# A row of reciprocals by TensorE, q scaled in PSUM, and five banks for the first words of the MLP

## The reference

```python
x   = x.reshape(4096, 512)                       # 2 batches of 2048 tokens
xn  = (x - mean(x)) / sqrt(var(x) + 1e-5)
q   = xn @ Wq.T + bq;  k = ctx @ Wk.T + bk;  v = ctx @ Wv.T + bv   # ctx: 2 x 77 x 512
a   = softmax(q k.T / sqrt(32)) v                # 16 heads of 32
x1  = x + tanh(g_xattn) * (a @ Wo.T + bo)
x1n = layernorm(x1)
sx  = max|x1n| / 127;  s1 = max|W1| / 127        # one scale per tensor
h   = gelu((round(x1n/sx) @ round(W1/s1).T + b1) * s1*sx)          # 2048 wide
sh  = max|h| / 127;   s2 = max|W2| / 127
out = x1 + tanh(g_ffn) * ((round(h/sh) @ round(W2/s2).T + b2) * s2*sh)
```

## Time and profile before

| | us |
|---|---|
| median of 3 runs | 666.09 |
| lowest and highest | 665.76 and 668.17 |
| the profiled execution | 664.78 |
| its span, first to last instruction | 662.6 |

### The profile page before, as it was taken

One profiled execution on the slowest core, in us unless ns is written; L12 is line 12 of the kernel. 1 busy time (PEld: TensorE's weight loads), 2 busy tenths in 40 slices (PEclk: granted clock), 3 DMA queues, 4 the chain that ended last, 5 costly groups with the idle time before them and its releaser, 6 DMA issues. The chain is left out here.

```text
span 662.6 us, 9249 instructions
## 1 busy us (share of the span) xinstructions
PE 593.2 (90%) x3289; PEld 336.4 (51%) x3311; DVE 452.0 (68%) x634; ACT 334.9 (51%) x400; POOL 288.6 (44%) x240
## 2 busy tenths in 40 slices
PE   6977869595998999969799997899999999999997
PEld 6832534452654746536457566544444454444443
DVE  5934861592784887827738688498999869893271
ACT  2445244463346364452462723577777669665440
POOL 3349366098076481872842522000000535843272
PEclk8997959796998999979989998999999999999999
DMA  8457020215321221121200103887777779797764
GB/s 316 155 194 236 1 80 1 47 64 175 125 97 35 47 97 35 32 80 47 96 1 0 66 0 137 302 307 279 285 267 276 321 317 320 282 403 307 240 232 181
DMA packets 45926, 107.42 MB, mean 162 GB/s; under 512 B 6976, under 2 KB 7744, under 8 KB 41280
## 3 DMA queue, kind: packets, MB, share of 16 engines
q1 hardware_dynamic: 44544, 105.55, 44.3%
q10 hardware_dynamic: 1344, 1.37, 0.6%
HBM read 64.95 MB, written 41.96 MB: 161 GB/s over the span
## 5 line engine op out<-in xcount | busy, mean ns | idle before, releaser
L1384 PE MATMUL ps<-h_sb,w_q 128*128 (+1 forms) x476 | 108.7, 379 | 2.4 <-ACT xo L1447 1.8
L1650 PE MATMUL ps<-w_q,h_q 128*128 128x512 bf16 x441 | 96.5, 379 | 0.4
L1108 POOL TENSOR_TENSOR xr<-xr,row 128x512 f32<-128x512 f32 x28 | 37.3, 1344 | 108.9 <-DMA xr<-in_x_t 89.2
L1732 POOL TENSOR_TENSOR xo<-xo,b2s 128x512 f32<-128x512 f32 x32 | 57.3, 1821 | 61.3 <-DMA xo<-x_dram 42.8
L1384 PEld LDWEIGHTS ps<-h_sb,w_q 128*128 128x128 bf16 x488 | 46.7, 98 | 53.9 <-ACT xo L1447 2.4
L684 ACT ACTIVATE prob<-ps 77x1024 f32<-77x1024 f32 x64 | 61.7, 1014 | 23.4 <-PE ps L466 18.9
L1650 PEld LDWEIGHTS ps<-w_q,h_q 128*128 128x128 bf16 x448 | 43.8, 98 | 52.9
L1447 ACT ACTIVATE xo<-ps,b1s,sc 128x1024 f32<-128x1024 f32 x48 | 57.6, 1204 | 20.0 <-PE ps L1384 19.0
L505 PE MATMUL ps<-wo_hi,c_lo 128*128 128x512 f32 x112 | 46.1, 412 | 23.6 <-POOL c_lo L1142 23.6
L1518 DVE TENSOR_REDUCE hmax<-xo 128x1024 f32 (+1 forms) x48 | 57.0, 1212 | 9.6 <-ACT xo L1447 9.4
L424 PE MATMUL ps<-xt_hi,wq_hi 128*128 128x512 f32 x128 | 53.2, 415 | 8.4 <-DVE x L913 7.7
(11 more groups left out here) (163 smaller groups left out, 1158.2 us busy)
## 6 DMA issues: line engine op xcount, KB each, us to landing
h_dram<-xo SPq DMA_DIRECT2D x48, 512.0 KB, 2.8
h_sb<-h_dram SPq DMA_DIRECT2D x16, 1024.0 KB, 11.1
x_dram<-x SPq DMA_DIRECT2D x8, 1024.0 KB, 4.1
xo<-x_dram SPq DMA_DIRECT2D x8, 1024.0 KB, 5.1
x<-h_dram SPq DMA_DIRECT2D x8, 1024.0 KB, 8.0
x<-in_x SPq DMA_DIRECT2D x7, 1024.0 KB, 5.6
xr<-in_x_t SPq DMA_DIRECT2D x28, 256.0 KB, 4.0
out<-xo SPq DMA_DIRECT2D x7, 1024.0 KB, 5.9
```

Source lines behind the costliest of these rows:

```text
L1108: nc.gpsimd.tensor_tensor(xa, xa, row[:], ALU.mult).then_inc(xr_mul, 1)
L1384: mm = nc.tensor.matmul(ps[:, 2 * (m % 2) + s, :], w1_q[:, k, m * P:(m + 1) * P], xq_t[:, one(2 * j + s), k, :], start=(k == 0), stop=(k = ...
L1650: mm = nc.tensor.matmul(ps[:, 4 * s + t, :], h_q[s][:, m, t * P:(t + 1) * P], w2_q[:, m, :], start=(m == 0), stop=(m == MF - 1))
L1732: nc.gpsimd.tensor_tensor(xo[:, s, t, :], xo[:, s, t, :], b2s[:], ALU.add).then_inc(xb_on, 1)
```

## The change

In attention:

- `pass_rstd`, the DRAM buffer and `scale_xt` are gone. TensorE's `row_turn(n)` turns the four columns of `rstd1`, broadcast, into a bank (`BC`, for n = 1 `BS`), in step n-1 behind the third `scores_by_token`. ScalarE's `row_copy(n)` copies the bank to `row`. `transpose_max` and, in step 0, the second half of v wait for that copy.
- x is split unscaled (`xt_high` waits for the DMA alone). VectorE's `q_scale(c, m)` multiplies the q in its PSUM bank by `row`, in place, before `q_high` and `q_low` read it. `divide(i-1, 0)` moves behind the last `token_max`.
- The maximum of w1 is turned by TensorE and reduced by VectorE, which does `w1_scale` before the residuals.
- In step 0 `weight_means` moves one place forward and ScalarE's copy of it from m = 1 to m = 0.
- A Gelu of one column stands in ScalarE's `last_steps`.

In hidden, the first eight tiles go through five banks, three are copied by VectorE; the last product of the last step, its Gelu and its maximum are done by halves. In output a factor that rounding doesn't need is computed after the first rounding.

```diff
-                def pass_rstd(c):
-                    sp.wait_ge(ln1_rstd, rstd_value(c))
-                    sp.dma_start(sh.rstd_dram[c].rearrange("(t p) -> p t", p=P), rstd1[:],
-                                 allow_slow_non_contiguous=True).then_inc(row_out, 16)
-                    sp.wait_ge(row_out, 16 * c)
-                    if c >= 2:
-                        sp.wait_ge(xr_mul, KD * (c - 1))
-                    sp.dma_start(row[:], as_row(sh.rstd_dram[c]).to_broadcast([P, CH])).then_inc(row_in, 16)
...
+                def row_turn(n):
+
+                    pe.wait_ge(ln1_rstd, rstd_value(n))
+                    if n >= 2:
+                        pe.wait_ge(c_on, GROUPS * (n - 1))
+                    for t in range(TT):
+                        mm = nc.tensor.transpose(ps[:, row_bank(n), t * P:(t + 1) * P],
+                                                 rstd1[:, t:t + 1].to_broadcast([P, P]), sh.ident[:])
+                    mm.then_inc(row_mm, 1)
...
                     if c == 0:
                         pe.wait_ge(v_on, 1)
+                    elif c < LAST:
+                        pe.wait_ge(row_on, c + 1)
...
+                    if i < LAST:
+                        row_turn(i + 1)
...
+                    if i == 1:
+                        pe.wait_ge(w1max_on, KD + 1)
+                        nc.tensor.transpose(ps[:, W1, 0:P], wmax[:, 0:1].to_broadcast([P, P]),
+                                            sh.ident[:]).then_inc(w1max_mm, 1)
...
+                def row_copy(n):
+                    act.wait_ge(row_mm, n)
+                    if n >= 2:
+                        act.wait_ge(q_scaled, scaled_count(n - 1, KD - 1))
+                    nc.scalar.copy(row[:], ps[:, row_bank(n), :]).then_inc(row_on, 1)
+
                 def xt_high(n, k):
                     act.wait_ge(q_mm, KD * n)
-                    act.wait_ge(xr_mul, xr_count(n, k))
+                    act.wait_ge(xr_in[k % 2], xr_value(n, k))
...
+                    nc.scalar.activation(bk_sb[:, 0:1], sh.bq[:, 0:1], ACT.Gelu)
...
+                def q_scale(c, m):
+                    dve.wait_ge(q_mm, KD * c + m + 1)
+                    dve.wait_ge(row_on, c)
+                    bank = ps[:, W0 if m % 2 == 0 else W1, :]
+                    nc.vector.tensor_tensor(bank, bank, row[:], ALU.mult).then_inc(q_scaled, 1)
...
+                    q_scale(i, 0)
                     q_low(i, 0)
                     reciprocals(i - 1)
+                    q_scale(i, 1)
                     token_max(i, 0)
                     q_low(i, 1)
-                    divide(i - 1, 0)
+                    q_scale(i, 2)
                     token_max(i, 1)
                     q_low(i, 2)
+                    q_scale(i, 3)
                     token_max(i, 2)
                     q_low(i, 3)
                     token_max(i, 3)
+                    divide(i - 1, 0)
                     divide(i - 1, 1)
...
-                def scale_xt(n, k):
-
-                    pool.wait_ge(xr_in[k % 2], xr_value(n, k))
-                    pool.wait_ge(row_in, 16 * n)
-                    xa = xr[:, k % 2, :]
-                    nc.gpsimd.tensor_tensor(xa, xa, row[:], ALU.mult).then_inc(xr_mul, 1)
...
-                        nc.gpsimd.partition_all_reduce(wmax[:, 1:2], wmax[:, 0:1], P, RMAX).then_inc(w1max_all, 1)
...
+        WORD_BANKS = (T0, T1, 1, 3, TW)
+        BY_DVE = (1, 3, 6)
...
+                    if u == TT - 1:
+                        copy_words(1)
+                        copy_words(3)
```

More of the change, by code:

```diff
@@ L21 @@
 AX = mybir.AxisListType
-RMAX = bass.bass_isa.ReduceOp.max
 P = 128
@@ L533, in first_step @@
                     scores_by_token(0, 0)
-                    weight_means()
                     project_q(0, 2)
                     scores_by_token(0, 1)
+                    row_turn(1)
                     project_q(0, 3)
@@ L1290, in hidden @@
         xqt_on = sem("xqt_on")
+        words_act = sem("words_act")
+        words_dve = sem("words_dve")
         h_mm = sem("h_mm")
@@ L1302, in one, with words_copied, words @@
             return j if isinstance(j, int) else bass.ds(j, 1)
+        WORD_BANKS = (T0, T1, 1, 3, TW)
+        BY_DVE = (1, 3, 6)
+        def words_copied(u):
+            by_dve = sum(v <= u for v in BY_DVE)
+            return (words_dve, by_dve) if u in BY_DVE else (words_act, u + 1 - by_dve)
+        def words(u):
+            return ps[:, WORD_BANKS[u % len(WORD_BANKS)], :].rearrange("p (k n) -> p k n", k=KD)
         def first_bank(m):
@@ L1381, in step @@
                             pe.wait_ge(h_on, MF * j + m - 1)
-                        for k in range(KD):
-                            for s in range(2):
-                                mm = nc.tensor.matmul(ps[:, 2 * (m % 2) + s, :], w1_q[:, k, m * P:(m + 1) * P],
-                                                      xq_t[:, one(2 * j + s), k, :], start=(k == 0),
-                                                      stop=(k == KD - 1))
+                        by_half = last and m == MF - 1
+                        for k, s in ([(k, s) for s in range(2) for k in range(KD)] if by_half else
+                                     [(k, s) for k in range(KD) for s in range(2)]):
+                            mm = nc.tensor.matmul(ps[:, 2 * (m % 2) + s, :], w1_q[:, k, m * P:(m + 1) * P],
+                                                  xq_t[:, one(2 * j + s), k, :], start=(k == 0),
+                                                  stop=(k == KD - 1))
+                            if by_half and k == KD - 1 and s == 0:
+                                mm.then_inc(h_mm, 1)
                         mm.then_inc(h_mm, 1)
@@ L1399, in _ @@
                 idle_turns(nc, sh, TW, 12)
-                for u in range(TT + 1):
+                for u in range(TT):
                     magic_words(u)
                 half(0, 0)
+                magic_words(4)
                 magic_words(5)
@@ L1426, in transposed @@
                     elif j == 0:
-                        words = ps[:, T0 if u % 2 == 0 else T1, :].rearrange("p (k n) -> p k n", k=KD)
-                        nc.scalar.activation(dst, words, ACT.Copy, bias=-MAGIC).then_inc(xqt_on, 1)
+                        nc.scalar.activation(dst, words(u), ACT.Copy, bias=-MAGIC).then_inc(words_act, 1)
                         return
@@ L1446, in step @@
                                 act.wait_ge(hmax_on, MF * j + m + 1 - RING)
+                        if last and m == MF - 1:
+                            nc.scalar.activation(dst[:, 0:CH], ps[:, bank, :], ACT.Gelu,
+                                                 bias=b1s[:, m:m + 1], scale=sc[:, 4:5]).then_inc(h_on, 1)
+                            act.wait_ge(h_mm, MF * j + m + 2)
+                            nc.scalar.activation(dst[:, CH:2 * CH], ps[:, bank + 1, :], ACT.Gelu,
+                                                 bias=b1s[:, m:m + 1], scale=sc[:, 4:5]).then_inc(h_on, 1)
+                            continue
                         nc.scalar.activation(dst.rearrange("p (s n) -> p s n", s=2),
@@ L1453, in _ @@
                 for u in range(PT):
-                    transposed(0, u)
+                    if u not in BY_DVE:
+                        transposed(0, u)
                 act.wait_ge(xs_on, 5)
@@ L1474, in _, with copy_words @@
                 dve.wait_ge(xs_on, 2)
+                def copy_words(u):
+                    dve.wait_ge(xqt_mm, u + 1)
+                    nc.vector.tensor_scalar(xq_t[:, u // TT, :, (u % TT) * P:(u % TT + 1) * P], words(u), -MAGIC, 1.0,
+                                            ALU.add, ALU.mult).then_inc(words_dve, 1)
                 for u in range(PT):
```

101 lines of the change are left out of this document (54 added, 47 removed).

## The result

The changed kernel takes **608.7 us** (median of four runs, 608.47 to 609.82) where the kernel before takes 665.92 on the same chip: a ratio of 0.914, 95% interval 0.911 to 0.917. The profiled execution has a span of 606.7 us against 662.6. The forecast was 614.3, with a range of 607 to 630; of the 5.6 us between them 4.1 are in the span (610.8 forecast), the rest in what the time has beyond its span. TensorE is busy for 95% of the span, VectorE for 77%; GpSimd's work fell from 288.6 to 247.7 us.

A forecast was written before the change was run, and what follows sets the result against it. TensorE was taken as the bound, with time to win only where it idles or runs slow. Gains of 59.8 less costs of 8.0 gave 51.8 net, span 662.6 to 610.8, hence 614.3 us, range 607 to 630.

The forecast's parts named there:

- `c_lo` wait of step 2: Sign of being right: no TensorE wait for `c_lo` above 2.5 us, and none outside step 2.
- Step 0: Attention's step 0: TensorE's 6.7 us wait for ScalarE's exponentials goes, 2.7 of slow clock returns; predicted gain 8.8.
- Step 1: Attention's step 1: the 5.9 us wait for `neg_max_t` goes, 1 us of clock returns; predicted gain 6.3.
- Steps 2 to 6: Attention: all 40.9 us of idle time and slower matmuls return, less 2.0 in step 2; predicted gain 34.4 after costs.
- w1's maximum: Step 2: TensorE's 7.7 us wait, hanging on VectorE's residuals behind GpSimd's maximum, goes; its transpose costs 0.3.
- The product on VectorE: Attention's q phase: 28 multiplications in the PSUM bank at 0.74 us each, priced by `q_lo`; slips 0.3 per step.
- rival C: Slower: multiplication within PSUM costs as much as the reciprocal from PSUM, 3.36 us; 687 us, chance 0.03.
- Rival A: VectorE becomes the bound of the q phase, at 1.08 us per multiplication; 622 to 629 us, chance 0.13.
- B: Divides take GpSimd's place: late `c_hi` keeps the `c_lo` waits of steps 3 to 6; 624 to 634 us, chance 0.07.
- D: `row_turn` waits for GpSimd's reciprocal, so the wait only moves to TensorE; 618 to 621 us, chance 0.03.
- Rival E: Start of hidden: transposes leave the clock low, costing 2 us more; 616 us, chance 0.01.
- Start of hidden: Up to hidden's first full step: early Gelu table load gains 1.28, five banks and VectorE copies 0.6; predicted 1.9.

The follow-up runs named there:

- the kernel before on C: The unchanged kernel before, profiled again on another chip than the result's: 657.6 us, span 655.5.

## Right and wrong, point by point

The time was 5.6 us under the forecast and inside its range, near the lower end. The mechanism was as forecast: the waits went, and with them the clock behind them. That the sum comes so near is in part luck, as several terms miss by 1 to 3 us and cancel. One of the signs that it named for being right failed: the `c_lo` wait of step 2 is 3.2 us, over its bound of 2.5.

- **Step 0** (8.8, measured 8.4): right.
- **Step 1** (6.3, measured 8.9): the wait of 5.9 went as said, and 3.8 us of idle time stay where 3.9 were forecast. The term that was mis-sized is the clock, "I give it back for 1 us only (0 to 3)": TensorE's busy time fell from 38.85 to 35.81, 3.0 us. That is luck too. The clock didn't fall at all in this execution; in others with the same step 1 it did, and the step took 40.5 or 41.9 us, a gain of 8.0 or 6.7. This is the stretch that misses most.
- **Steps 2 to 6** (34.4, measured 34.7): right in sum, by terms that cancel. "All waits go" holds in steps 3, 5 and 6, and they take 38.64 where 39.6 was forecast; step 4 has a new wait of 1.24. Two terms were too dear. The turned row was put at 0.6 us a step, the price of four turns by themselves; the steps without it are 0.2 shorter, as the turns overlap with the matmuls around them. VectorE's slips of 0.3 a step are nothing, as the phase has 1 us left; with 2.8 - 1.45 = 1.3 us put in, it had some 2.3 before (an estimate) and not "about a microsecond". Two were too cheap. In step 2, "1.5 to 2.5 us of wait are left, and with some clock I take 2.0": the wait was 3.24, and behind it the clock was at 0.57 for 4 us, so the step took 5.0 more than its neighbours:

```profile
119.70:123.80 4.10, 0.86 (x7) 0.30 (x3) 3.85 (x10) 0.30 (x1) 4.10 (x4) 1.00 0.28 79
123.80:127.80 4.00, 4.00 (x29) 1.53 (x33) 2.50 (x8) 2.88 (x5) 3.96 (x6) 0.57 0.90 300
```

  And in step 4 the split of k, ahead of the products of q, cost 1.4 (40.1 against 38.7 us with the split moved and undisturbed), which no term of the sum had.
- **The cause in step 2** was named rightly, GpSimd's conversion of w1 and bias; moving the bias alone removes all of the wait.
- **w1's maximum** (7.7 as a term of the 40.9): alone it is worth 5.4. Waits of one step were added as if they were independent. The sum came out right because all of them were removed at once. What the maximum is worth within the whole change was not measured.
- **The product on VectorE** (0.74 by the nearest row, measured 0.694): right, and rival C (2.6 and more) is out.
- **Rival A** didn't come about, but for step 4, where the split of k used up the room and TensorE waited 1.24 us for the maxima. It was nearer than it looked: 1 us of room per step, and every further product costs 0.4 to 0.7. Had the product taken the 1.08 of the rival, 4 x 0.39 = 1.5 more a step would have left 0.5 over the room, seven times. **B** and **D** are out: TensorE waits neither for `c_hi` nor for the row.
- **Rival E**: the clock rises in the start of the hidden stage with nothing but turns running, 3.3 us after its first (0.56, then 1.00), earlier than before, where it was still at the lower level at 416 to 417, 4.3 to 5.3 us in. When it rises is a matter of the moment and not of the change. These are the first profile of the changed kernel, then the kernel before on C (its first turn at 405.45), then the run with the split of k and GpSimd held back (at 353.61):

```profile
361.00:363.00 2.00, 2.00 (x12) 2.00 (x11) 1.90 (x7) 0.00 (x0) 0.00 (x0) 0.56 0.85 275
363.00:364.00 1.00, 1.00 (x11) 1.00 (x10) 0.38 (x1) 0.32 (x1) 0.00 (x0) 1.00 1.01 375
409.20:410.20 1.00, 0.84 (x8) 0.60 (x6) 0.56 (x2) 0.56 (x2) 0.00 (x0) 1.00 0.91 319
353.61:358.61 5.00, 5.00 (x24) 5.00 (x25) 2.78 (x9) 0.25 (x1) 0.26 (x1) 0.50 0.73 231
```

- **Start of hidden** (1.9, measured 3.2): table 1.28 (measured 1.27, right), banks and copies 0.6 (measured 0.97, too low); the rest, about 0.95, is that earlier rise, which the run with the old hidden stage has too. It is luck: the changed stage starts in 14.0 to 15.4 us in nine profiles, the old one in 16.2 to 17.2 in four. The drain of about 1.38 us that the Trainium skill, ScalarE: Activation LUTs, What ACT_TABLE_LOAD costs, gives beside the load doesn't show: the load starts 0.02 us after ScalarE's instruction ahead of it, and ScalarE goes on 0.01 us after its end.

```profile
331.13 0.59 ACT L714 COPY c_sb<-ps 128x512 f32<-128x512 f32 x1 [1.27 <-PE ps L480]
331.74 1.28 ACT L814 ACT_TABLE_LOAD   x1
333.03 0.20 ACT L814 ACTIVATE bk_sb<-bq_sb 128x1 f32<-128x1 f32 x1
```

- **End of hidden** 0.6 (0.57 and 0.74), **output** 0.1: right.

## What to carry to other kernels

Find the cheap instruction that waits for something late in an in-order queue, and ask what stands behind it: here 37 us of multiplication on a GpSimd that was idle more than half of the time cost TensorE over 20 us of waits, and twice that when the row they wait for came later. When a part is moved to another engine, measure the room there by doing it twice; when it is moved beside GpSimd, look whether both read SBUF. Waits of one step are often one delay seen at several places: their sum is the gain only if all of them are removed. A forecast to 1% of such a kernel hangs on when the clock falls and rises, and single executions differ by more than its smaller terms.

## What the runs showed of the hardware

- A product in place in a PSUM bank, 128x512 in float32 by a row in SBUF, takes VectorE 0.694 us, less than `q_lo`'s 0.742, 675 to 700 ns in the changed kernel's profile. A subtraction of 32x308 from SBUF to SBUF takes 0.47 us, and up to 1.50 beside GpSimd's additions.
- Four turns of 128x128 within a stream of matmuls make a step 0.2 us longer (38.65 against 38.45), not 0.6.
- After the same idle time the granted clock sometimes stays at 1.00 and sometimes falls to half, in one and the same program: 39.6 or 40.5 us for step 1 (41.9 in a run that differs only behind it). Behind 3.8 us of idle time at the start of the hidden stage, with turns alone running, it was back at 1.00 after 3.3 us in one profile and still at 0.50 after 5.0 in another.
- The row's 2 KB write to DRAM took a median of 8.2 to 9.2 us to land in four profiles, more than reading 256 KB back (5.1 to 5.5).
